# Score rows of two heads on two halves of the partitions, and max rows carried by small DMAs

## The reference, cut to what matters

```
qkv = layernorm(x) @ W_attn                       # 16 heads of 8 channels
q, k = rope(q), rope(k)
att = softmax(causal(q @ k.T / sqrt(8)))          # 8 batches x 16 heads of 512 x 512
x = x + (att @ v) @ W_proj
gates = sinkhorn(layernorm(x) @ gate_w)           # 8 iterations
each expert takes its 64 best tokens of a batch; its output counts where the gate is over 0.5
x = x + routed outputs of the experts
```

## Time and profile before

| | |
|---|---|
| median of 3 runs | 553.28 us |
| the profiled execution | 556.51 us, of which its span 554.8 |
| mean granted TensorE clock | 0.915 |
| start up to the first score row | 42.6 us |
| the 32 steps | 50.3 to about 419 us |
| PE, DVE, ACT, POOL busy | 78%, 76%, 60%, 42% of the span |
| DMA | 36.7 MB, mean 66 GB/s |

### The profile page before, as it was taken

The page is one execution under the profiler, slowest core; times in us unless marked ns, Lnnn a source line. Parts: engine busy times, 40 slices in busy tenths (PEclk is TensorE's granted clock), DMA queues, the critical chain, the costliest instruction groups (busy, mean ns, idle before and its releaser), DMA issues.

```text
span 554.8 us, 11459 instructions
## 1 busy us (share of the span) xinstructions
PE 432.3 (78%) x2985; PEld 219.7 (40%) x2985; DVE 419.3 (76%) x1693; ACT 331.3 (60%) x660; POOL 232.2 (42%) x399
## 2 busy tenths in 40 slices
PE   0507989989998898998989899899987778898200
PEld 0202445454554445445444554545543333343100
DVE  7777668778878768877867887778951699889980
ACT  0002568677868657877775887768693324328613
POOL 5121453363365236336424633633342000009997
PEclk9955879999999989999999999989999799899755
DMA  8570052035026004402600520360010100101111
GB/s 255 138 180 0 30 158 44 1 115 135 2 94 136 22 0 141 105 1 95 151 2 28 152 66 0 114 132 2 2 58 0 40 19 19 39 0 38 39 45 48
DMA packets 28108, 36.72 MB, mean 66 GB/s; under 512 B 2072, under 2 KB 24088, under 8 KB 26392
## 3 DMA queue, kind: packets, MB, share of 16 engines
q1 hardware_dynamic: 27120, 34.68, 22.7%
q10 hardware_dynamic: 944, 1.57, 1.1%
HBM read 19.41 MB, written 16.78 MB: 65 GB/s over the span
## 4 chain that ended last, share of the span: by engine, by line
PE 54%; DVE 13%; ACT 10%; POOL 10%; issue 9%; DMA 2%; DVEq 1%; POOLq 1%; ACTq 1%
PE ROWB L446 12%; PE PVB L471 12%; PE CHB L459 11%; PE MB L505 5%; PE MB L479 5%; ACT YS L702 4%; POOL SUM L848 4%; POOL SUM L846 3%; PE MB L515 3%; PE MB L494 3%; PE ROWB L643 2%; ACT XN L681 1%; DVE XN L946 1%; DMA parts_scratch<-PARTS 1%; POOL SUM L850 1%
## 5 line engine op out<-in xcount | busy, mean ns | idle before, releaser
L895 DVE CUSTOM_DVE_ANT_0 JUNK<-ROWB,TRI 128x384 bf16<-128x384 f32 (+3 forms) x512 | 221.2, 487 | 41.0 <-PE ROWB L446 39.6
L702 ACT ACTIVATE YS<-CHB 128x512 f32<-128x512 f32 x320 | 171.9, 607 | 56.9 <-PE CHB L459 56.8
L812 POOL TENSOR_SCALAR_AFFINE_SELECT YS<-YS 128x256 f32<-128x256 f32 x256 | 104.6, 413 | 178.7 <-ACT YS L702 170.1
L446 PE MATMUL ROWB<-YS 96*128 96x384 bf16 (+3 forms) x512 | 123.4, 314 | 24.0 <-DMA YS<-parts_scratch 17.7
L459 PE MATMUL CHB<-YS 100*128 100x384 bf16 (+3 forms) x512 | 118.3, 308 | 12.9 <-ACT YS L702 11.0
L471 PE MATMUL PVB<-YS,VP 128*32 128x512 f32 (+3 forms) x1024 | 97.0, 452 | 0.2 <-POOL YS L812 0.2
L446 PEld LDWEIGHTS ROWB<-YS 96*128 96x128 bf16 x512 | 43.3, 100 | 101.6 <-DVE MX L895 57.2
L459 PEld LDWEIGHTS CHB<-YS 100*128 100x128 bf16 x512 | 46.3, 100 | 48.0 <-ACT YS L702 19.4
L656 ACT ACTIVATE YS<-MB 4x1024 bf16<-4x1024 bf16 x32 | 32.5, 1017 | 38.6 <-PE MB L494 38.5
L771 ACT ACTIVATE YS<-YS,W 128x128 f32<-128x128 f32 x104 | 31.5, 388 | 35.6 <-POOL SUM L846 18.9
L846 POOL TENSOR_TENSOR SUM<-YS 128x512 f32<-128x512 f32 x13 | 16.9, 1298 | 70.1 <-ACT YS L771 70.1
(11 more groups left out here) (124 smaller groups left out, 568.7 us busy)
## 6 DMA issues: line engine op xcount, KB each, us to landing
YS<-parts_scratch SPq DMA_DIRECT2D x30, 384.0 KB, 6.4
parts_scratch<-PARTS SPq DMA_DIRECT2D x15, 384.0 KB, 2.5
parts_scratch<-PARTS SPq DMA_DIRECT2D x15, 256.0 KB, 2.2
X<-in_x SPq DMA_DIRECT2D x8, 256.0 KB, 5.7
xn_scratch<-XN2S SPq DMA_DIRECT2D x8, 256.0 KB, 2.0
XS<-xn_scratch SPq DMA_DIRECT2D x8, 256.0 KB, 2.6
out<-X SPq DMA_DIRECT2D x8, 256.0 KB, 2.3
parts_scratch<-PARTS SPq DMA_DIRECT2D x15, 128.0 KB, 1.7
```

The lines of the kernel that those rows point to most:

```text
L446: last = pe.matmul(ROWP[BANK[u]][:, col:col + keys], QP[par][0:ROWS_K, pair, P * qb:keys], KZ[par][i % 2][0:ROWS_K, pair, 0:keys], start=T ...
L702: act.activation(PT[s % 2][:, c, :], CH[BANK[c]], ACT.Exp).then_inc(exp_done, 1)
L812: pool.affine_select(out=v, in_=v, pattern=[[0, 2], [1, P]], compare_op=ALU.is_ge, fill=0.0, base=0, channel_multiplier=-1).then_inc(causa ...
L895: last = dve.tensor_tensor_reduce(out=JUNK[BANK[u]][:, col:col + n], in0=ROWP[BANK[u]][:, col:col + n], in1=TRI[:, T - n:T], scale=1.0, sc ...
```

## The change

**Rows.** The zeros go. KZ becomes KP, one copy for each of the two buffers. The first head of a pair has rows 0 to 47, the second rows 64 to 111 (HALF = 64), in QP and in KP. A unit's matmul contracts over 48 rows from row 0 or row 64 (it was 96 from row 0), a chunk's over 50 (it was 100). Head i's half is i % 2; the last two units and chunks are regrouped (heads i and i + 2), so that each has one half. Before each such matmul group that waits for a bank, PE executes a nop that carries the wait.

**Max rows.** The maxima are stored in another order, so that four PE transposes of eight columns give 8 x 512 values in rows 0 to 7 of MB. ACT copies these to MXR (two buffers), and SP moves them with two DMAs of four 1 KB rows each to rows 48, 49 and 112, 113 of QP (`load_max`). c0 waits for these DMAs (max_loaded). In SP's program they stand among the parts' stores and loads: those of steps 0 and 1 ahead of the next batch's stores, that of step 2 between stores and loads, that of step 3 behind the loads.

**Order.** STEP and the tables are written anew. The four memsets of KZ are gone.

```diff
-ROWS_K = 2 * HEAD_ROWS
-MAX_ROW = ROWS_K
-ALL_K = MAX_ROW + 4
+HALF = P // 2
+MAX_ROW = HEAD_ROWS
+ALL_K = MAX_ROW + 2
-STEP = [("w", 8), ("n", 0), ("n", 1), ("v", 0), ("u", 0), ("w", 9), ("x", 0), ("u", 1), ("u", 2),
...
+STEP = [("n", 0), ("n", 1), ("w", 6), ("w", 7), ("mx", 0), ("u", 0), ("u", 1), ("v", 0), ("w", 8), ("w", 9),
+        ("x", 0), ("u", 2), ("u", 3), ("v", 3), ("x", 1), ("c", 0), ("c", 1), ("v", 1), ("u", 4), ("u", 5),
+        ("v", 2), ("c", 2), ("c", 3), ("x", 2), ("u", 6), ("u", 7), ("c", 4), ("c", 5), ("ot", 0), ("x", 3),
+        ("u", 8), ("u", 9), ("x", 4)]
-EXTRAS = {(0, 1): "xnT n", (0, 2): "q n", (0, 3): "qs n", (0, 4): "k n", (1, 0): "ks n",
+EXTRAS = {(0, 0): "xnT n", (0, 1): "q n", (0, 2): "qs n", (0, 3): "k n", (0, 4): "ks n",
-CUT = {(1, "x", 0): (0, 0), (1, "v", 1): (1, 0), (1, "c", 1): (1, 1), (1, "u", 6): (0, 1),
-       (1, "x", 3): (1, 2)}
+CUT = {(0, "x", 4): (0, 0), (1, "w", 7): (1, 0), (1, "x", 0): (0, 1), (1, "x", 1): (1, 1), (1, "c", 1): (0, 2)}
+CUT_V = {(1, "x", 2): (1, 2)}
+NORMALIZE = (0, "w", 6)
...
+            def load_max(bt, s):
+                sp.wait_ge(misc_free, bt.misc(f"mx{s}") + 1)
+                for h in range(2):
+                    r = HALF * h + MAX_ROW
+                    sp.dma_start(QP[bt.par][r:r + 2, 2 * s:2 * s + 2, :],
+                                 MXR[s % 2][4 * h:4 * h + 4, :]).then_inc(max_loaded, 16)
...
                 if not isinstance(b, int) or n >= BACK[u]:
                     pe.wait_ge(row_max, n + 1 - BACK[u])
+                    pe.nop(nofuse=True)
                 for qb, i, col in UNITS[u]:
-                    last = pe.matmul(ROWP[BANK[u]][:, col:col + keys], QP[par][0:ROWS_K, pair, P * qb:keys],
-                                     KZ[par][i % 2][0:ROWS_K, pair, 0:keys], start=True, stop=True)
+                    last = pe.matmul(ROWP[BANK[u]][:, col:col + keys], QP[par][r:r + HEAD_ROWS, pair, P * qb:keys],
+                                     KP[par][r:r + HEAD_ROWS, pair, 0:keys], start=True, stop=True)
...
                 if c == 0:
-                    pe.wait_ge(misc_free, bt.misc(f"mx{s}") + 1)
+                    pe.wait_ge(max_loaded, 32 * (4 * b + s + 1))
...
-                for j in range(2):
-                    for qb in range(TB):
-                        col = T * j + P * qb
-                        last = pe.transpose(MBH[MAX_ROW:MAX_ROW + 4, col:col + P],
-                                            NMX[:, 2 * qb + j, :, :].rearrange("p h n -> p (h n)"), IDB[:, :])
+                for qb in range(TB):
+                    last = pe.transpose(MBH[0:8, P * qb:P * qb + P],
+                                        NMX[:, 2 * qb:2 * qb + 2, :, :].rearrange("p h n j -> p (h n j)"), IDB[:, :])
...
-                take(bt, f"mx{s}", QP[par][MAX_ROW:MAX_ROW + 4, 2 * s:2 * s + 2, :].rearrange("p a t -> p (a t)"),
-                     MBH[MAX_ROW:MAX_ROW + 4, :])
+                take(bt, f"mx{s}", MXR[s % 2][:, :], MBH[0:8, 0:T])
...
-            for i in range(2):
-                pool.memset(KZ[i][1][:, :, :].rearrange("p a t -> p (a t)").bitcast(U32), 0).then_inc(built, 1)
...
-            dve.memset(KZ[0][0][:, :, :].rearrange("p a t -> p (a t)").bitcast(U32), 0).then_inc(built, 1)
-            dve.memset(KZ[1][0][:, :, :].rearrange("p a t -> p (a t)").bitcast(U32), 0).then_inc(built, 1)
```

More of the change, by code:

```diff
@@ L70 @@
 UNITS = [[(3, i, 0)] for i in range(4)] + [[(2, i, 0), (0, i, 3 * P)] for i in range(4)] + \
-        [[(1, 2 * i, 0), (1, 2 * i + 1, 2 * P)] for i in range(2)]
+        [[(1, i, 0), (1, i + 2, 2 * P)] for i in range(2)]
 NU = len(UNITS)
 CHUNKS = [[(i, 0, 0)] for i in range(4)] + [[(i, 1, 0), (i, 3, 3 * P)] for i in range(4)] + \
-         [[(2 * i, 2, 0), (2 * i + 1, 2, 2 * P)] for i in range(2)]
+         [[(i, 2, 0), (i + 2, 2, 2 * P)] for i in range(2)]
 NC = len(CHUNKS)
@@ L171, in arena @@
             return v
-        KZ = [[arena([P, PAIRS, T], BF16) for h in range(2)] for i in range(2)]
+        KP = [arena([P, PAIRS, T], BF16) for i in range(2)]
         QP = [arena([P, PAIRS, T], BF16) for i in range(2)]
         PT = [arena([P, NC, T]) for i in range(2)]
-        assert STORED * E * C <= taken[0] <= 22 * E * C
+        assert taken[0] <= 22 * E * C
         WQKV = sb("WQKV", [P, 3 * C])
@@ L208, in build @@
         MX = [sb(f"MX{i}", [P, 16]) for i in range(2)]
-        NMX = sb("NMX", [P, 8, 2, 2], BF16)
+        NMX = sb("NMX", [P, TB * 2, 2, 2], BF16)
+        MXR = [sb(f"MXR{i}", [8, T], BF16) for i in range(2)]
         JUNK = [sb(f"JUNK{i}", [P, T], BF16) for i in range(3)]
@@ L352, in load_rows @@
             for h in range(2):
-                rows = (QP[par] if w == 0 else KZ[par][h])[:, :, :].rearrange("p a t -> p (a t)")
-                queue.dma_start(rows[HEAD_ROWS * h:HEAD_ROWS * h + HEAD_ROWS, :],
+                rows = (QP, KP)[w][par][HALF * h:HALF * h + HEAD_ROWS, :, :]
+                queue.dma_start(rows.rearrange("p a t -> p (a t)"),
                                 scratch[w, par, :, :, h].rearrange("s d a t -> (s d) (a t)")).then_inc(loaded[w], 16)
@@ L389, in one @@
                         store_part(sp, bt.b + 1, 1 - bt.par, w, n)
+                load_max(bt, 2)
+                if bt.nxt:
                     if bt.prev:
@@ L453, in chunk @@
                 if c == 0:
-                    pe.wait_ge(misc_free, bt.misc(f"mx{s}") + 1)
+                    pe.wait_ge(max_loaded, 32 * (4 * b + s + 1))
                 if not isinstance(b, int) or n >= BACK[c]:
                     pe.wait_ge(exp_done, n + 1 - BACK[c])
+                    pe.nop(nofuse=True)
                 for i, kb, col in CHUNKS[c]:
-                    pair, n = 2 * s + i // 2, T - P * kb
-                    last = pe.matmul(CH[BANK[c]][:, col:col + n], KZ[par][i % 2][0:ALL_K, pair, P * kb:P * kb + P],
-                                     QP[par][0:ALL_K, pair, P * kb:T], start=True, stop=True)
+                    pair, n, r = 2 * s + i // 2, T - P * kb, HALF * (i % 2)
+                    last = pe.matmul(CH[BANK[c]][:, col:col + n], KP[par][r:r + ALL_K, pair, P * kb:P * kb + P],
+                                     QP[par][r:r + ALL_K, pair, P * kb:T], start=True, stop=True)
                 last.then_inc(chunk_ready, 1)
@@ L702, in exps, with max_rows_taken @@
                 act.activation(PT[s % 2][:, c, :], CH[BANK[c]], ACT.Exp).then_inc(exp_done, 1)
-            def max_rows_taken(bt, par, s):
-                take(bt, f"mx{s}", QP[par][MAX_ROW:MAX_ROW + 4, 2 * s:2 * s + 2, :].rearrange("p a t -> p (a t)"),
-                     MBH[MAX_ROW:MAX_ROW + 4, :])
+            def max_rows_taken(bt, s):
+                if not isinstance(bt.b, int) or 4 * bt.b + s >= 2:
+                    act.wait_ge(max_loaded, 32 * (4 * bt.b + s - 1))
+                take(bt, f"mx{s}", MXR[s % 2][:, :], MBH[0:8, 0:T])
             def values_taken(b, s):
@@ L751, in copy_outputs @@
                 act.activation(YS[:, E * C * n:E * C * n + E * C], EXPB[n % 2], ACT.Copy).then_inc(y_copied, 1)
-            exps(B - 1, 3, 8)
-            exps(B - 1, 3, 9)
+            for c in range(6, NC):
+                exps(B - 1, 3, c)
             values_taken(B - 1, 3)
@@ L836, in _ @@
             batches(pool, one)
-            causal(B - 1, 3, 6)
-            causal(B - 1, 3, 7)
+            for z in range(4, NZ):
+                causal(B - 1, 3, z)
             rstd(B, ln2_stats, MV2, RSTD2[:, :], SHIFT2[:, :], ln2_rstd)
```

39 lines of the change are left out of this document (21 added, 18 removed), and 3 rows, old and new, of the table STEP.

## The result

The changed kernel takes 678.7 us (median of 4 runs, 674.4 to 680.0) against 553.8 us for the kernel before on the same chip (4 runs, 551.2 to 555.5). The ratio is 1.225, with a 95% interval of 1.217 to 1.232. The prediction was 571 us, with a range of 530 to 602. The sign was right, the size off by 108 us.

What follows compares the result with a forecast made beforehand. DVE was taken as the floor, its 8.8 us idle a batch as the room for gain. From 553.3 us, +18 for the batches, -4 at the start and +4 for the clock gave 571 us, range 530 to 602.

Steps and rivals of the forecast that it cites:

- The order and its max rows: Per-batch sum: max rows by DMA make u4 late, less PE's relief; +2.4 us a batch, +18 us over 7.5 batches.
- The clock: PE's granted clock over the run: +4 us, or 32 us if it falls once a step.
- Rival B: PE idle ahead of c0 and its work pressed together lower the clock once a step: 599 us; chance 0.14.
- The relief of PE: Paired half-height matmuls overlap: up to 1.5 us of PE a step; counted 0.1 us plain, 0.3 to 0.4 in steps 0 and 1.
- Rival C: The pairs of matmuls don't overlap: 10 us more, 581 us; chance 0.09.
- rival A: The relief pays, with max rows landing a microsecond sooner: -1.8 us a batch, 538.5 or 535 us; chance 0.27.
- SP: Next batch's loads wait 2.7 us more behind step 2's max rows; hidden by c0's wait, counted at nothing.
- The head of the step: Step's start: n1 ends T+0.4, four transposes until T+0.9; T is the step's start.
- The chain to c0: Transposes, copy and DMAs of max rows: c0 at T+4.0, u4 to DVE at T+5.45 where it was T+4.24.
- The start: First normalization (XN) and statistics without the four memsets: first score row sooner, -4 us.
- The change of kind: PE going from one kind of matmul to another, as chunks to values: 0.1 us each, a rule against the change.

Runs made afterwards that it cites:

- i2: i1 without the empty instructions behind TensorE's waits: 619.5 us.
- i1: h1 with c0 waiting only for ScalarE's copy, the max rows' DMAs going to rows that nothing reads: 626.1 us.
- e1: Changed kernel with units over partition rows 0 to 111 and chunks over 0 to 113 in place of one half: 654.5 us.
- k2: j1 with c0 waiting for the max rows' DMAs again, these placed ahead of the row loads: 659.4 us.
- k1: Changed kernel with the maxima's transposes moved behind u0, u1 and v0, and without the empty instructions: 705.5 us.
- g1: e1 with STEP and its tables as in the kernel before: 645.2 us.
- f1: Changed kernel, halves and DMAs kept, with STEP and its tables as in the kernel before: 692.4 us.
- j3: Kernel before at full height, with the empty instructions and pairing of heads i and i+2 that e2 and f2 have: 560.1 us.
- f2: e2 with all matmuls of units and chunks on the same rows, 0 to 47, so none can overlap: 646.4 us.
- e3: Changed kernel with c0 waiting only for ScalarE's copy, the max rows' DMAs writing to rows that nothing reads: 671.1 us.
- j1: i2 with the maxima's transposes moved behind u0, u1 and v0: 582.2 us.
- e2: Kernel before with its unit and chunk matmuls cut to one half of the partitions, last ones pairing heads i and i+2: 647.6 us.
- j2: e2 with its chunks back at full height, only the units on one half: 643.8 us.

## Why the prediction was wrong, point by point

Three steps of it failed. The order and its max rows stood at +18 us. At full height, with the clock nearly back, the change costs 101 us all the same: PE idles at the head of the step (a wait that the sum doesn't hold, worth 37 us), the row loads and the max rows get in each other's way on SP (counted at nothing, 28 us together with the wait at c0), the empty instructions cost 7 us, and 29 us stay open. The clock stood at +4 us; the halves cost 24 us on top of that, and 86 us where nothing else holds PE up.

The terms of the 125 us, along one path through the runs (each the difference of two medians):

| step | us |
| --- | --- |
| kernel before, 553.5, to the new order at full height, c0 waiting for no DMA, no empty instructions (i2) | +66 |
| the empty instructions (i1 less i2) | +7 |
| c0 waits for the DMAs, and the row loads stand behind step 2's max rows (e1 less i1) | +28 |
| the halves (changed kernel less e1, which also starts 5 us later for its memsets) | +24 |

The terms don't add independently. Height costs 24 (e1), 46 (k2 to k1), 47 (g1 to f1) and 86 us (j3 to f2), the first three in truth 4 to 6 us more, by which their full-height kernels start later. This fits that a slow clock costs the more, the less PE waits for others.

- **The clock** was mis-sized. It stood at +4 us with a bound of 32, from the one sort of fall that the trace of before had, after idle time (1.0 us a fall). The mean granted clock fell to 0.741, and the prediction had named 0.85 as the point where this step fails. The bound was no bound: it priced one short fall a step, and step 3 lay at 0.50 throughout in two batches. (The part at 0.50 in the earlier trace rows, from 193.70 us, belongs to another step 0 than the one of 13.53 us above it; that one has such a part from about 289 to 292.5 us, so the price stands. The traces give the clock as a share of full speed only: what the prediction calls 1.2 GHz is their 0.50, at which the 512 columns of a unit took 0.43 us in f2 (227.43 to 227.86 us), 1.2 columns a nanosecond.) What the trace of before could not show is that the change takes away what held the clock, the height of its matmuls: 96 and 100 rows of 128.
- **Rival B** had the right quantity and the wrong cause. It gave 599 us for PE idling at c0. Without that wait (e3) the clock stayed at 0.743.
- **The relief of PE** is real as instructions: pairs run side by side in all their parts, more than the forecast allowed (u4 and u5, four matmuls, take 0.40 us at full clock; at full height 0.61, in e1). By the two pages units and chunks take 184.6 us in place of 241.7; but at the lower clock the values take 135.4 in place of 97.0. Rival C is out; rival A, too.
- **SP** is another step that failed. "The last landed before u0 of step 3 [...] If it is late, c0's wait in that step hides it. I count nothing; without that cover it is 1 us a batch." In e1, at full height, PE waited 2.65 us at u0, long before c0, and lost its clock with it. Away from the loop's edge e1's step 3 takes 16.0 to 17.0 us, where the forecast had 10.6, and i1's 11.7.
- **The head of the step.** The forecast put the transposes at T+0.5 and saw only DVE's wait. It did not ask what PE does between u9 and T+0.5: nothing, 1.5 to 1.8 us a step, 42.7 us in i2. Undone in j1, it gave 37 us.
- **The chain to c0** was about right: forecast T+4.0, found T+4.55 with a slow v0 ahead of it, and T+4.11 in e1 at full clock; u4 came to DVE at T+6.93, in e1 at T+5.96, rather than 5.45. In e1 at full clock steps 2, 0 and 1 took 10.94, 15.64 and 15.29 us against forecasts of 10.6, 14.4 and 12.7. On the mean of batches 1 to 6 the forecast comes to 49.6 us (47.2 + 2.4) and the changed kernel took 64.0. Of the 14.4 us between them 10.8 are already in e1 (60.5), about 6 of these in step 3, and 3.5 come with the halves.
- **The start**: first minus_max at 46.42 in place of 50.29, -3.9 us for a forecast of -4, and XN done at 11.3 us, as "by 12 us" had it.
- **The change of kind** stood at 0.1 us, as a reason to expect less of the relief; it is in no sum, and no run separates it. The row behind it, 0.32 us, gives only the sum of 512 columns and a change; that 512 columns need about 0.22 us shows elsewhere in that trace (a unit at 229.91 us, the chunk behind it at 230.13). Halves cost the same without any overlap (f2, 86 us over j3) and with it (e2, 87 us).

Left open: what halving the units alone costs (j2); whether it is the number of rows or something else that sets the short ones apart; whether the max rows on another engine's queue than SP's would be on time, which no run tried; and what the order at full height still costs over the kernel before when nothing waits and the transposes are late (j1, 29 us; its step 0 of 15.02 against 12.51 is the largest part).

## What to carry to other kernels

A full-height matmul with zeros in half of its rows was not waste here: it held TensorE's clock (0.98 in j3 against 0.79 in f2). Before cutting a contraction in two and running the halves side by side, cut the rows alone in the old kernel (as e2 and f2 do, whatever values come out) and read the granted clock. A wait that is costed at nothing because another one hides it must be placed in time first. Here the row loads' wait came before the one that was to hide it. And with two kinds of DMA on one queue, one large and one tiny and urgent, neither order had both on time (PE waited 2.65 us for the large one in e1, 4.13 us for the tiny one in h1).
